# Second layers of two expert quarters in a row on TensorE, with the gates multiplied in place in four tiles

## What is computed

```python
t = tokens                                   # normalised, 64 channels
out = t
for e in range(8):
    h = gelu(t @ w1[e] + b1[e])              # first layer, 64 -> 64
    y = h @ w2[e] + b2[e]                    # second layer, 64 -> 64
    out = out + combine[:, e:e + 1] * y      # combine: 0 for six of the eight experts
```

## Time and profile before

| | |
|---|---|
| median of 3 runs | 1255.58 us (1255.0 to 1255.82) |
| the profiled execution | 1252.18 us |
| its span in the trace | 1250.3 us |
| PE busy | 1136.2 us, 91% of the span |
| DVE busy | 1017.2 us, 81% |
| ACT busy | 670.9 us, 54% |
| TensorE clock granted, mean | 0.927 of full speed |

### The profile page before, as it was taken

One profiled execution on the slowest core, in us unless ns is written; L12 is line 12 of the kernel. 1 busy time (PEld: TensorE's weight loads), 2 busy tenths in 40 slices (PEclk: granted clock), 3 DMA queues, 4 the chain that ended last, 5 costly groups with the idle time before them and its releaser, 6 DMA issues.

```text
span 1250.3 us, 27967 instructions
## 1 busy us (share of the span) xinstructions
PE 1136.2 (91%) x8762; PEld 785.6 (63%) x8762; DVE 1017.2 (81%) x3482; ACT 670.9 (54%) x1183; POOL 211.5 (17%) x217
## 2 busy tenths in 40 slices
PE   7868988898889999888876999999999999999998
PEld 7747877777677878776664555555555555555554
DVE  6948889999999999999987877777777777777775
ACT  0026665555556555555643655555555555555553
POOL 5013333333333333333331000000000000000000
PEclk9959898889988788889985999999999999999999
DMA  9401111111111111111100111111111111121111
GB/s 329 154 16 39 47 54 49 46 45 44 45 37 52 41 48 43 46 44 45 37 23 30 30 46 47 48 46 49 44 44 44 44 47 48 45 51 44 44 44 37
DMA packets 127771, 66.15 MB, mean 53 GB/s; under 512 B 111104, under 2 KB 125696, under 8 KB 126944
## 3 DMA queue, kind: packets, MB, share of 16 engines
q1 hardware_dynamic: 119024, 52.26, 16.0%
q10 hardware_dynamic: 8064, 12.85, 2.7%
q0 software_dynamic: 624, 0.43, 0.2%
HBM read 39.81 MB, written 25.69 MB: 52 GB/s over the span
## 4 chain that ended last, share of the span: by engine, by line
PE 48%; DVE 40%; POOL 5%; issue 4%; ACT 2%; DMA 1%; POOLq 0%; SPq 0%; DVEq 0%; ACTq 0%
PE p L1074 15%; PE p L1049 14%; PE p L1059 9%; DVE tn_s L775 7%; DVE xn_s L760 6%; DVE t_s L766 6%; POOL t_s L406 5%; DVE st L720 4%; DVE arena L614 3%; DVE sm L734 2%; PE p L901 2%; PE p L1070 2%; PE p L894 1%; DMA resid<-in_x_dram 1%; PE p L1034 1%
## 5 line engine op out<-in xcount | busy, mean ns | idle before, releaser
L822 DVE TENSOR_TENSOR arena<-arena,p 128x896 f32<-128x896 f32 x224 | 243.6, 1087 | 129.1 <-PE p L1059 124.3
L539 ACT ACTIVATE arena<-p,b_s 128x896 f32<-128x896 f32 x224 | 225.0, 1005 | 229.6 <-PE p L1049 229.6
L1074 PE MATMUL p<-arena,w_s 128*64 128x448 f32 x896 | 215.7, 560 | 0.3 <-DVE arena L822 0.3
L1049 PE MATMUL p<-thl,w_hi 128*128 128x448 f32 x448 | 165.4, 450 | 0.5 <-DVE thl L796 0.5
L1059 PE MATMUL p<-arena,selector 128*128 128x448 bf16 x448 | 124.4, 359 | 3.4 <-DVE arena L822 2.9
L1049 PE MATMUL p<-thl,w_lo 128*128 128x448 f32 x448 | 127.1, 365 | 0.0
L1059 PEld LDWEIGHTS p<-arena,selector 128*128 128x128 bf16 x448 | 25.4, 97 | 161.4 <-issue 116.1
L398 POOL TENSOR_TENSOR yb<-yb,bet 128x448 f32<-128x448 f32 x56 | 63.6, 1135 | 274.1 <-DVE xn_s L760 274.1
L1017 PE MATMUL p<-arena 128*96 128x128 f32 x784 | 106.5, 276 | 0.0
L1017 PEld LDWEIGHTS p<-arena 128*96 128x96 f32 x784 | 101.3, 168 | 3.8
L1049 PEld LDWEIGHTS p<-thl,w_hi 128*128 128x128 f32 x448 | 85.6, 192 | 21.2 <-issue 0.8
(11 more groups left out here) (164 smaller groups left out, 2043.6 us busy)
## 6 DMA issues: line engine op xcount, KB each, us to landing
tn_spill<-tnt_s ACTq DMA_DIRECT2D x56, 224.0 KB, 1.9
arena<-tn_spill SPq DMA_DIRECT2D x56, 224.0 KB, 3.4
arena<-in_x_dram SPq DMA_DIRECT2D x112, 96.0 KB, 2.1
out_dram<-arena SPq DMA_DIRECT2D x112, 96.0 KB, 1.8
resid<-in_x_dram SPq DMA_DIRECT2D x6, 1568.0 KB, 12.8
resid<-in_x_dram SPq DMA_DIRECT2D x6, 384.0 KB, 6.3
arena<-in_x_dram SPq DMA_DIRECT2D x112, 16.0 KB, 2.0
out_dram<-arena SPq DMA_DIRECT2D x112, 16.0 KB, 1.7
```

Of the source, the lines that this page charges most:

```text
L539: a.activation(hid[:, j % 2, :].rearrange("p (h n) -> p h n", h=H), (p34 if j % 2 == 0 else p56)[:, :, 0:CH], ACT.Gelu, bias=b1_s[:, j:j + ...
L822: v.tensor_tensor(gated[:, j % 2, :].rearrange("p (h n) -> p h n", h=H), hid[:, j % 2, :].rearrange("p (h n) -> p h n", h=H), p01[:, :, 0: ...
L1049: last = t.matmul(bank[:, h, 0:CH], w[:, 128 * j:128 * (j + 1)], thl[:, c, h, :], start=(k == 0), stop=(k == 1))
L1074: last = t.matmul(p2[64 * h:64 * h + 64, 0:CH], w2_s[:, j, :], gated[:, j % 2, h * CH:(h + 1) * CH], start=False, stop=(j == 3))
```

## The change

`gated` goes; `hid` has four slots, one a quarter, and the gate multiplies in place. A gelu now waits for the second layer of the same quarter in the group before (`s_l2`, u - 3) instead of a multiplication, and the multiplication waits for no second layer. PE's step is written anew: the second layers stand in two pairs, and the spread of quarter 3 moves to the start of the next step. The steps of DVE and ACT keep their order.

```diff
-        hid = carve(at3, [2, H * CH])
-        gated = carve(at3, [2, H * CH])
+        hid = carve(at3, [4, H * CH])
...
             def gelu(g, c, j):
                 u = g * 4 + j
                 wait(act, s_h, u + 1)
-                wait(act, s_gm, u - 1)
-                a.activation(hid[:, j % 2, :].rearrange("p (h n) -> p h n", h=H),
+                wait(act, s_l2, u - 3)
+                a.activation(hid[:, j, :].rearrange("p (h n) -> p h n", h=H),
...
                 wait(dve, s_g, u + 1)
                 wait(dve, s_c, u + 1)
-                wait(dve, s_l2, u - 1)
-                v.tensor_tensor(gated[:, j % 2, :].rearrange("p (h n) -> p h n", h=H),
-                                hid[:, j % 2, :].rearrange("p (h n) -> p h n", h=H),
+                v.tensor_tensor(hid[:, j, :].rearrange("p (h n) -> p h n", h=H),
+                                hid[:, j, :].rearrange("p (h n) -> p h n", h=H),
                                 p01[:, :, 0:CH], ALU.mult).then_inc(s_gm, 1)
...
             def step3(g, c, has, more=True, first=0):
-                for j in range(4):
-                    if has(0) and j >= first:
+                if has(1):
+                    spread(g - 1, 1 - c, 3)
+                if has(0):
+                    for j in range(first, 2):
                         first_layer(g, c, j)
-                    if j == 3 and has(0) and more:
+                    spread(g, c, 0)
+                if has(1):
+                    second_layer(g - 1, 1 - c, 2)
+                    second_layer(g - 1, 1 - c, 3)
+                if has(0):
+                    spread(g, c, 1)
+                    first_layer(g, c, 2)
+                if has(1):
+                    back(g - 1, has(0))
+                if has(0):
+                    first_layer(g, c, 3)
+                    spread(g, c, 2)
+                    if more:
                         comb_t(g + 1, 1 - c)
-                    if j < 2:
-                        if has(1):
-                            second_layer(g - 1, 1 - c, j + 2)
-                    else:
-                        if j == 2 and has(1):
-                            back(g - 1, has(0))
-                        if has(0):
-                            second_layer(g, c, j - 2)
-                    if has(0):
-                        spread(g, c, j)
+                    second_layer(g, c, 0)
+                    second_layer(g, c, 1)
```

More of the change, by code:

```diff
@@ L1073, in second_layer @@
                 for h in range(H):
-                    last = t.matmul(p2[64 * h:64 * h + 64, 0:CH], w2_s[:, j, :], gated[:, j % 2, h * CH:(h + 1) * CH],
+                    last = t.matmul(p2[64 * h:64 * h + 64, 0:CH], w2_s[:, j, :], hid[:, j, h * CH:(h + 1) * CH],
                                     start=False, stop=(j == 3))
```

## The result

The changed kernel takes 1271.3 us (median of 4 runs, 1270.6 to 1273.75), the kernel before 1255.47 us beside it. The ratio is 1.0137 with an interval of 1.0124 to 1.0150: **1.4% slower**. Timed again with the experiments, it took 1270.7 us against 1254.59, 1.0134 (1.0117 to 1.0151). The prediction had said 1271.4 us, slower, and named the wait.

What follows compares the result with a forecast made beforehand. The prediction took PE's list to bound stage 3; the new order closes a loop with DVE at 0.28 us more a group. 15.1 + 1.1 - 0.4 = +15.8 us on 1255.58 gave 1271.4 us, range 1261 to 1284.

Steps and rivals of the forecast that it cites:

- PE bounds stage 3 and its list counts 56 times: Stage 3: PE busy 100.00 of 100 us, so its list of 10.02 us a group sets the time, 56 times.
- the 105.7 us of the earlier trace: Stage 3 before: read as PE's time waiting for nothing that shows, ahead of spreads, 0.70 us each.
- The new list would take 9.81 us if it never waited: PE's regrouped list per group: 9.81 us against 10.02, a gain of 0.21 us.
- The wait at `comb_t`: PE must wait for DVE's `finish`: `comb_t` starts 3.78 us after P1, 0.52 later than PE could.
- The loop of 10.30 us: Closed path over PE and DVE, P1 to next P1: 10.30 us against 10.02, 0.28 us more a group.
- Edits costed at nothing: Multiplying in place, the gelu's new wait, the multiplication's dropped wait and gate 3 before P0: no cost.
- Edges, +0.7 us: Routing on the loop in groups 1 and 2, +1.1 us; first and last group without stall, -0.4 us.
- The sum of +15.8 us: Whole kernel: 15.1 us for 54 groups with the wait, +1.1 and -0.4 at the edges.
- the wait stays hidden: Rival at `comb_t`: only the drains count, the list's 0.21 us gain shows 56 times, 1243.8 us; chance 0.08.
- A second wait on the loop: Rival: P0 waits for gate 3, or gate 0 is late behind its gelu; 1277 to 1286 us; chance 0.18.
- Neighbours worth more than taken: Rival: inner second-layer pairs take 0.30 us instead of 0.37, change comes out even, 1253 to 1259 us; chance 0.06.

Runs made afterwards that it cites:

- finish_first: Changed kernel with two calls swapped on DVE, `finish` of the group before ahead of `low`: 1243.97 us, 0.9915 of the kernel before.
- comb_last: Changed kernel with `comb_t` on PE behind the second layers of quarters 0 and 1 instead of ahead of the bias: 1238.89 us, 0.9873 of the kernel before.
- back_joined: Changed kernel with `comb_t` behind the second layers of quarters 0 and 1, and `back` moved behind the spread of quarter 2: 1223.26 us, 0.9744 of the kernel before.
- tiles_only: Kernel before with four `hid` slots, multiplication in place and the gelu's new wait, PE's order as before: 1254.68 us, 0.9998 of the kernel before.

## Why the prediction was right, step by step

- *PE bounds stage 3 and its list counts 56 times*: right. Without the wait, a shorter list came out as shorter time in finish_first, comb_last and back_joined. One reading was off: the 105.7 us of the earlier trace rows are idle time of the weight loads (PEld), not of PE, which was busy all the time. A row that was not shown puts 35.2 us more, ahead of P1, down to DVE's multiplication. Nothing in the sum hangs on it.
- *The new list would take 9.81 us if it never waited*: 9.85 measured in finish_first. From P1 to `comb_t` 3.28 us for the 3.26 summed up; S0 and S1 1.61 for 1.60; P3' to S2' 904.77 - 902.29 = 2.48 for 2.48. The first full-width products behind the flips, which no row had shown, cost what was taken for them (flips to F3 0.26 us, F3 to P2 0.92). The items of that stretch, though, add up to 1.70 us and not to the 1.64 that the prediction wrote: it took 0.21 us for the flips, where the earlier trace rows have 0.17. The trace has 1.66, so the slip did no harm by luck.
- *The wait at `comb_t`*: right in place, cause and size. P1 to `comb_t` is 906.43 to 910.22, 3.79 us for 3.78. The release cost 0.15 us as in the earlier trace rows.
- *The loop of 10.30 us*: it is 10.34. Summed from the rows above: 3.79 from P1, 0.39 and 0.40 for `comb_t` and bias, 1.61, 2.48, 1.66, together 10.33. The excess is a hundredth of a us in each of several terms; no term failed.
- *Edits costed at nothing*: right for the tiles, the place of the multiplication and the gelu's wait (tiles_only). P0 doesn't wait: P3' to P0 is 2.00 us, the length of its full-width matmuls.
- *Edges, +0.7 us*: the first four intervals, with routing and a table load in the third, grew from 43.8 to 45.8 us, 2.0 in sum, one by one by -0.24, 0.80, 0.54 and 0.89. The prediction's terms give -0.21, 0.84, 0.84 and 0.28, together 1.75. So the sum is near, and one term was left out: group 3 has routing operations between gate 1 and `low` too, and `comb_t` came 4.63 us after P1 there. At the end of the stage the 0.2 us that the last group was to win did not show (5.21 us from its P1 to its P3 before, 5.29 after).
- *The sum of +15.8 us*: in the profile stage 3 grew by 18.1 us (562.4 to 580.5): 51 intervals of 0.316 and the 2.0 of the first four. The medians differ by 15.8. So the total is as near as it is partly by luck: the stage was undercounted by 2.3 us, 1.8 of it in the 0.04 us per group, and the rest of the program came out 2 us shorter in these runs.
- *Rivals*: that the wait stays hidden (1244 us) fell, and finish_first at 1243.97 us is what it would have been. A second wait on the loop didn't come. Neighbours worth more than taken: no, the inner pairs ran at 0.37 us as taken; the 0.12 us of comb_last are not in them but in the way out of S1.

The Trainium skill's rule that a change of the tiling mode drains the engine (TensorEngine Tiling, Key Properties) agrees with these traces as far as they go: going into half-width work cost 0.09 us and the way out 0.10, and fewer blocks of it took less time as long as PE had no wait. The traces show the time, not the drain itself. Taken alone the rule gave the wrong sign for this change.

## What to carry to other kernels

Grouping PE's half-width products saves a piece per block, here 0.17 us (10.02 to 9.85, four blocks to three) and 0.31 us (9.73 to 9.41, three to two) a group, and each regrouping moves other work earlier against engines that didn't move. So measure for every wait on PE how late its releaser is, in us after the PE instruction that started the releaser's chain, and compare it with PE's new path; spare time in the old order (0.68 us) is what the regrouping may use up (it took 1.05). If a chain on a second engine starts at PE and ends at PE, that engine's idle share says nothing; look for another order on either engine. Here one swap of two calls on DVE turned 1.4% slower into 0.9% faster. With DVE's order left alone, moving `comb_t` on PE gave 1.3% faster, and moving `back` too gave 2.6%.

## What the runs showed of the hardware that was not expected

- The order inside one half-width block matters: `comb_t` (bf16, 64 and 32 columns) at the end of the block instead of at its start saved 0.12 us a group (9.85 to 9.73), as the second layers then have no full-width products behind them.
- A wait of 0.5 us in every 10 us on PE left the granted clock at 1.00, in the changed kernel from 692.5 to 1264 us.
- Multiplying in place took 1088 ns, into another tile 1087 ns (128 x 896, one operand in PSUM).
